# A 17-tap convolution with three outputs from five products over pairs of batches, and the last scaling of a layer norm on ScalarE

## The chip, the cores and the metric

One Trainium2 chip, one core of it. The metric is the time of one execution of the kernel on the device in microseconds, median of three runs. TensorE (PE in the rows) multiplies matrices and writes PSUM; VectorE (DVE), ScalarE (ACT) and GpSimd (POOL) work element by element; SyncE (SP) issues the transfers. Each engine takes its own instructions strictly in the order in which they are written, and they meet through semaphores.

## What is computed

Sixteen graphs (batches) of 512 nodes with 128 channels go through two layers. The first, cut to what matters here:

```
xc = x.T                                     # per batch 128 x 512
h  = relu(bn1(conv1x1(xc)))
h  = bn2(conv1d(h, conv2_w, 17 taps, padding 8))     # 128 -> 128 channels
x_conv = relu(h + xc).T
s = x @ w_se.T + b_se                        # 3 columns
A = exp(-|s_n - s_m|^2) * adj                # 512 x 512
x_nmp = A @ relu(x @ w_msg.T + b_msg)
gi = [x_conv, x_nmp] @ w_ih.T + b_ih ; gh = x @ w_hh.T + b_hh
r, z = sigmoid(gi_r + gh_r), sigmoid(gi_z + gh_z)
g  = (1 - z) * tanh(gi_n + r * gh_n) + z * x
x  = layernorm(x + g)
```

The second layer, five small graph convolutions, touches only the first 25 nodes of each batch; they are worked off together near the end.

## The kernel before

Everything is kept transposed, channels on the 128 partitions and the 512 nodes along the free side. Products that must be exact to nearly fp32 are made of three: each operand is split into a high part (`_h`, rounded by a copy on ScalarE) and a low part (`_l`, the rest, a subtraction on VectorE), and `mm3` adds high·high, high·low and low·high in PSUM.

The 17-tap convolution makes two neighbouring outputs from four products. `first_conv` writes relu(bn1(...)) into `h1`; `differences` and `sums_differences` make `dd` (528 columns) and `sd` (1056 columns) from its even and odd columns, which are split into `_h` and `_l`. `conv_part` multiplies them with the taps, grouped by three: four parts of 6, 5, 6 and 6 groups, so 23 x 3 = 69 matmuls of 256 columns for each batch, into the halves of `p_outer` and `p_middle`. ScalarE brings the middle parts to `mid`, VectorE makes `cu` from `p_outer` and the input (`outer_sum`), and then `cv` (`conv_sum`), two operations on every other column and one on all.

`first` works off batch 0 and prepares batch 1. Then come fifteen steps, written with one function `step` for each engine: batch 1, a loop of three rounds over the batches 2 to 13, and batches 14 and 15. In step b the engines finish the gates and the layer norm of batch b-1 while TensorE works on batch b. On TensorE a step is: the convolution's `p_outer` parts, in odd steps the six `rows` matmuls that serve two batches, `conv1` and `msg` of batch b+1, the first middle part, four transposes of the result of b-1, the second middle part, twelve matmuls with the masked `am` (the neighbour product), then 27 gate matmuls of 512 columns in three groups of nine: those that use x, those that use the neighbours (`n_h`, `n_l`) and those that use the convolution (`c_h`, `c_l`), with the four `dist` matmuls of b+1 put between them. `rt`, `zt` and `nn` are tanh on ScalarE; `gg`, `tt`, `ya`, `yb`, `y2` on VectorE combine them.

On VectorE the layer norm of b-1 is `stats`, `moments` (which also makes `base`), and `normalise`: one small operation for `x1`, which keeps the first nodes for the second layer, and four of 128 columns that write `yo`, (yn - mean) * rs. `rs` is a power made by GpSimd (`powers`). After `normalise` come the four `mask` operations. SyncE stores `yo` and then, in the same queue, issues the four loads of `adj` for batch b+2, and in the next step the load of `xin` for three batches ahead. `right` is filled by a transfer from `left` (`rows_left`) once for two batches.

## Time and profile before

| | us |
|---|---|
| median of 3 runs (387.93 to 392.32) | 389.65 |
| the profiled execution | 387.58 |
| its span in the trace | 385.8 |
| TensorE busy | 367.9 |
| VectorE busy | 348.9 |
| ScalarE busy | 227.6 |
| GpSimd busy | 38.9 |

The span runs from the first instruction to the last. A matmul stands in the trace from its start to the modelled end of its last column, and the next one starts meanwhile; so the distance between the starts of neighbouring matmuls is what one costs, and a full share of TensorE says little by itself. Short operations of the other engines overlap a little in the same way. An entry such as `<-ACT am_h` names what an engine waited for.

### The profile page before, as it was taken

What the parts mean: (1) busy time and instruction counts of PE and PEld (TensorE: products, weight loads), DVE (VectorE), ACT (ScalarE), POOL (GpSimd) and SP (SyncE); (2) the same over time, 40 slices, a digit from 0 to 9 for tenths busy, and PEclk for the clock granted to TensorE, in tenths of its full rate; (3) what the DMA queues carried; (4) which work ended last, traced back from release to release, by engine and by line L of the source; (5) the groups of instructions that cost most, each with busy time, mean ns of one, the idle gap of its engine ahead of it and who ended that gap; (6) DMA issues with size and microseconds to landing.
All of it is one profiled execution on the core that took longest, in us unless ns stands there. A gap on an engine that the chain in (4) does not pass through costs nothing.

```text
span 385.8 us, 7010 instructions
## 1 busy us (share of the span) xinstructions
PE 367.9 (95%) x2259; PEld 319.9 (83%) x2259; DVE 348.9 (90%) x719; ACT 227.6 (59%) x353; POOL 38.9 (10%) x54
## 2 busy tenths in 40 slices
PE   4799999999999999999999999999999999899994
PEld 2687988989797989889898979898898979687783
DVE  4998999999999999999999999999999999975746
ACT  5573756575656665655756666666657564644350
POOL 7000030100101010101001010101010060111013
PEclk9999999999999999999999999999999999999999
DMA  8662405050231405050403114050504003000100
GB/s 224 205 194 81 138 11 165 1 159 14 61 108 31 134 12 163 0 163 10 136 27 111 52 37 137 0 163 10 163 0 145 23 11 130 2 27 2 33 29 22
DMA packets 27342, 30.23 MB, mean 78 GB/s; under 512 B 3098, under 2 KB 16338, under 8 KB 27322
## 3 DMA queue, kind: packets, MB, share of 16 engines
q1 hardware_dynamic: 26860, 29.87, 25.2%
q8 instruction: 10, 0.16, 0.2%
q10 hardware_dynamic: 462, 0.12, 0.1%
q14 instruction: 10, 0.08, 0.1%
HBM read 24.84 MB, written 4.40 MB: 76 GB/s over the span
## 4 chain that ended last, share of the span: by engine, by line
PE 66%; DVE 18%; issue 9%; ACT 4%; DMA 1%; DVEq 0%; POOLq 0%; SPq 0%; ACTq 0%; POOL 0%
PE p_outer L605 14%; PE ring L605 14%; PE p_middle L605 9%; PE p_r L605 8%; PE p_z L605 7%; PE p_gi L605 7%; PE p_gh L605 5%; DVE sd_l L1134 3%; DVE st L1172 2%; DVE n_l L1210 2%; DVE sd L1130 1%; DVE sd L1129 1%; ACT rows L861 1%; DVE m_l L1143 1%; DVE dd L1120 1%
## 5 line engine op out<-in xcount | busy, mean ns | idle before, releaser
L605 PE MATMUL p_middle<-sd_h,w_h 128*128 128x256 f32 x192 | 56.8, 296 | 0.0
L605 PE MATMUL p_middle<-sd_h,w_l 128*128 128x256 f32 x192 | 54.3, 283 | 0.0
L605 PE MATMUL p_middle<-sd_l,w_h 128*128 128x256 f32 x192 | 54.0, 281 | 0.0
L1072 POOL TENSOR_TENSOR rs<-base,cst 128x5 f32<-128x5 f32 x16 | 20.0, 1249 | 325.6 <-DVE base L1183 325.6
L605 PE MATMUL p_outer<-dd_h,w_l 128*128 128x256 f32 x176 | 49.4, 281 | 0.0
L605 PE MATMUL p_outer<-dd_h,w_h 128*128 128x256 f32 x176 | 49.4, 280 | 0.0
L605 PE MATMUL p_outer<-dd_l,w_h 128*128 128x256 f32 x176 | 49.3, 280 | 0.0
L886 ACT ACTIVATE am<-ring 128x512 f32<-128x512 f32 x56 | 33.3, 595 | 19.4 <-PE ring L605 18.9
L1149 DVE TENSOR_TENSOR am<-am,adj 128x512 f32<-128x512 f32 x64 | 40.9, 683 | 1.3 <-ACT am L886 1.3
L1306 DVE TENSOR_TENSOR am_l<-am,am_h 128x2048 fp32r<-128x2048 f32 x15 | 34.4, 2292 | 3.3 <-ACT am_h L981 3.2
L605 PEld LDWEIGHTS p_middle<-sd_h,w_h 128*128 128x128 f32 x192 | 36.4, 189 | 0.3 <-issue 0.2
L605 PEld LDWEIGHTS p_middle<-sd_l,w_h 128*128 128x128 f32 x192 | 36.3, 189 | 0.2 <-issue 0.2
L605 PEld LDWEIGHTS p_middle<-sd_h,w_l 128*128 128x128 f32 x192 | 36.3, 189 | 0.0
L605 PEld LDWEIGHTS p_outer<-dd_l,w_h 128*128 128x128 f32 x176 | 33.3, 189 | 0.6
L605 PEld LDWEIGHTS p_outer<-dd_h,w_h 128*128 128x128 f32 x176 | 33.2, 189 | 0.7
L605 PEld LDWEIGHTS p_outer<-dd_h,w_l 128*128 128x128 f32 x176 | 33.1, 188 | 0.0
L605 PE MATMUL ring<-right,left 128*128 128x512 f32 x62 | 26.0, 422 | 6.1 <-DVE n_l L1210 4.1
L981 ACT ACTIVATE am_h<-am 128x2048 fp32r<-128x2048 f32 x15 | 28.5, 1902 | 0.0
L900 ACT ACTIVATE c_h<-cv 128x512 fp32r<-128x512 f32 x16 | 10.1, 633 | 24.8 <-DVE cv L1206 24.8
L605 PE MATMUL ring<-am_h,m_l 128*128 128x512 f32 x60 | 23.5, 392 | 0.0
L605 PE MATMUL ring<-am_l,m_h 128*128 128x512 f32 x60 | 23.5, 392 | 0.0
L605 PE MATMUL ring<-am_h,m_h 128*128 128x512 f32 x60 | 23.5, 392 | 0.0
(297 smaller groups left out, 959.8 us busy)
## 6 DMA issues: line engine op xcount, KB each, us to landing
adj<-adjT SPq DMA_DIRECT2D x64, 256.0 KB, 3.4
xin<-xT SPq DMA_DIRECT2D x17, 256.0 KB, 3.0
out<-yo SPq DMA_DIRECT2D x16, 256.0 KB, 2.5
gw<-g_w SPq DMA_DIRECT2D x2, 640.0 KB
wc<-w_c SPq DMA_DIRECT2D x2, 384.0 KB, 4.6
right<-left SPq DMA_DIRECT2D x15, 48.0 KB
wg<-w_ih SPq DMA_DIRECT2D x1, 384.0 KB, 5.6
wc<-w_c SPq DMA_DIRECT2D x1, 320.0 KB, 4.0
```

The source lines that it names most:

```text
L605: return nc.tensor.matmul(out_, w, x, start=start, stop=stop, skip_group_check=True)
L861: A(ab, p_gh[:], ACT.Identity, bias=rowb[:, 0:1], scale=cst[:, C_ROW:C_ROW + 1]).then_inc(s_ab, 1)
L886: A(am[:, c, :], R_D[c][:], ACT.Exp).then_inc(s_e[c], 1)
L900: A(c_h[:], cv[:], ACT.Relu).then_inc(s_ch, 1)
L981: A(am_h[:], am[:], ACT.Copy).then_inc(s_amh, 1)
L1072: TT(rs[:], base[:], cst[:, C_MH:C_MH + CH + 1], ALU.pow).then_inc(s_rs, 1)
L1120: TT(dd[:], halves(h1, 0), halves(h1, 2), ALU.subtract).then_inc(s_dd, 1)
L1134: TT(sd_l[:], sd[:], full(sd_h[:]), ALU.subtract).then_inc(s_sdl, 1)
L1149: TT(am[:, c, :], am[:, c, :], adj[:, c, :], ALU.mult).then_inc(s_am[c], 1)
L1172: last = nc.vector.bn_stats(st[:, c, :], yn[:, c, :])
L1210: TT(n_l[:], R_NMP[:], full(n_h[:]), ALU.subtract).then_inc(s_nl, 1)
L1306: TT(am_l[:], am[:], full(am_h[:]), ALU.subtract).then_inc(s_aml, 1)
```

## The change

It has two parts.

The first: each five products give three outputs, for two batches at once. `h1` holds two batches side by side. VectorE makes from it five streams of 2 x 178 columns: `neighbour_steps` (712 columns) and `second_steps` (1068) take differences, `inner` (712) makes streams 1 and 2, `outer` (712) streams 0 and 4, and stream 3 is read from the second differences directly; ScalarE copies the high parts (712, 712 and 356 columns) and VectorE subtracts the low parts (`inner_low`, `outer_low`, `middle_low`). `stream` multiplies: 6, 6, 6, 6 and 5 groups of three taps, three matmuls each, 87 matmuls of 2 x 172 = 344 columns for a pair. Two streams are multiplied in the odd step, three in the even step after it, so that odd and even steps have functions of their own. Out of PSUM, ScalarE writes `ev`; VectorE makes `pq` (`first_sums`, 2 x 344 columns, in the odd step), `vv` (`second_sums`, 3 x 344), adds the input on all three phases (`add_input`, 1026 columns with a stride of three) and two more phases of 342 columns (`add_first`, `add_last`). `c_h` and `c_l` are made for both batches at once (1024 columns). In odd steps `conv1` is done for two batches, and the convolution's gate matmuls stand before those of the neighbours. In the first batch, `first` makes both batches' streams and all five products, with a fifth set of weights, three of them sums of taps; `add_input` is spread over other operations there. Buffers are laid over one another: `t_raw` over `ya`, `yb` and `y2`, `cv` over `rt` and `zt`, `gw1` over the old taps, which is now loaded in the last step.

The second: the four operations that write `yo` move from VectorE's `normalise` to ScalarE, as Identity with a scale `rs` and a bias `nb` for each partition. GpSimd makes `nb` = -(mean * rs) with two operations more after its power. On ScalarE they stand at the end of a step, behind `gates`; in the last step ahead of them.

The diff, cut to its core; of the step functions of TensorE, ScalarE and VectorE only the new text and kept lines are shown, in that order:

```
 G3 = (TAPS + 1) // 3
-PH = HALF + PAD
+TILE3 = (N + 2) // 3
+N3 = 3 * TILE3
+NM = TILE3 + 1
+J3 = NM + G3
+W3 = 3 * J3
+XS = N3 + 1
...
+def window(t, at, g):
+    return t[:, at, :].rearrange("p (b j) -> p b j", b=2)[:, :, g:g + NM]
+def stream(k, to):
+    w_h, w_l = (w0_h, w1_h, w2_h, w3_h, w4_h)[k], (w0_l, w1_l, w2_l, w3_l, w4_l)[k]
+    at = (2, 0, 1, 4, 3)[k]
     count = w_h.shape[1]
     for g in range(count):
-        par, i = (3 * g + first) % 2, (3 * g + first) // 2
-        last = mm3(out_, w_h[:, g, :], w_l[:, g, :], v_h[:, par, i:i + HALF], v_l[:, par, i:i + HALF],
+        last = mm3(both(to, NM), w_h[:, g, :], w_l[:, g, :], window(t_h, at, g), window(t_l, at, g),
                    g == 0, g == count - 1)
-    return last
...
+    after(pe, s_t3h, n.pair(1)); after(pe, s_t3l, n.pair(1))
+    after(pe, s_ev, n.pair(1))
+    stream(3, p_outer)
+    after(pe, s_e[3], n(1))
+    msg(q, R_MSG)
+    after(pe, s_t04h, n.pair(1)); after(pe, s_t04l, n.pair(1))
+    after(pe, s_pq, n.pair(1))
+    stream(0, p_middle)
+    turn(n)
+    after(pe, s_v, n.pair(1))
+    stream(4, p_outer)
+    after(pe, s_mt, n(2))
+    neighbour_product(0, n)
+    after(pe, s_rt, n(0)); gate(p_r, "r", 2, xb_h, xb_l, True, False)
+    after(pe, s_zt, n(0)); gate(p_z, "z", 2, xb_h, xb_l, True, False)
+    after(pe, s_ghb, n(0)); gate(p_gh, "n", 2, xb_h, xb_l, True, True).then_inc(s_gx, 1)
+    after(pe, s_left, n.pair(1)); after(pe, s_right[1], n.pair(1) * 16)
+    after(pe, s_yn, n(0))
+    dist(q, 0)
+    after(pe, s_nh, n(1)); after(pe, s_nl, n(1))
+    dist(q, 1)
+    gate(p_r, "r", 1, n_h[:], n_l[:], False, False)
+    after(pe, s_e[0], n(2))
+    dist(q, 2)
+    gate(p_z, "z", 1, n_h[:], n_l[:], False, False)
+    after(pe, s_tt, n(0)); gate(p_gi, "n", 1, n_h[:], n_l[:], True, False)
+    after(pe, s_e[1], n(2))
+    dist(q, 3)
+    after(pe, s_ch, n.pair(1)); after(pe, s_cl, n.pair(1))
+    gate(p_r, "r", 0, cb_h, cb_l, False, True).then_inc(s_gr, 1)
+    gate(p_gi, "n", 0, cb_h, cb_l, False, True).then_inc(s_gi, 1)
+    gate(p_z, "z", 0, cb_h, cb_l, False, True).then_inc(s_gz, 1)
...
+    cb_h, cb_l = c_h[:, 1, :], c_l[:, 1, :]
     more = not static(b, B - 1)
     if static(b, B - 1):
+        pe.wait_ge(s_w0, PAIRS); pe.wait_ge(s_w2, PAIRS)
         g_pe.spread(pe, mm)
+    if more:
         after(pe, s_xh, n(3)); after(pe, s_xl, n(3)); after(pe, s_ghb, n(0))
         rows(v + 1)
+        after(pe, s_w0, n.pair(0)); after(pe, s_pq, n.pair(0))
+        conv1(q, p_middle)
+        after(pe, s_w2, n.pair(0))
+        conv1(r, p_outer)
         after(pe, s_e[3], n(1))
         msg(q, R_MSG)
+    after(pe, s_rt, n(0))
+    gate(p_r, "r", 2, xb_h, xb_l, True, False)
+    gate(p_r, "r", 0, cb_h, cb_l, False, False)
+    after(pe, s_zt, n(0))
+    gate(p_z, "z", 2, xb_h, xb_l, True, False)
+    gate(p_z, "z", 0, cb_h, cb_l, False, False)
+    after(pe, s_tt, n(0))
+    gate(p_gi, "n", 0, cb_h, cb_l, True, False)
     if static(b, B - 1):
         g_pe.combine(pe, mm)
+    if more:
+        after(pe, s_val, n.pair(1))
+    after(pe, s_ghb, n(0)); gate(p_gh, "n", 2, xb_h, xb_l, True, True).then_inc(s_gx, 1)
+    turn(n)
+    if more:
+        after(pe, s_mt, n(2))
     else:
+        after(pe, s_e[3], n(1))
+    neighbour_product(1, n)
     if static(b, B - 1):
         pe.wait_ge(s_msel, 2)
         pe.wait_ge(s_grow, B - 2)
         for i in EARLY:
             g_pe.aggregate(pe, mm, i)
+    if more:
+        after(pe, s_t12h, n.pair(1)); after(pe, s_t12l, n.pair(1))
+        after(pe, s_h1, n(3))
+        stream(1, p_outer)
+        after(pe, s_left, n.pair(1)); after(pe, s_right[0], n.pair(1) * 16)
         after(pe, s_yn, n(0))
         dist(q, 0)
+        stream(2, p_middle)
     after(pe, s_nh, n(1)); after(pe, s_nl, n(1))
     if more:
         dist(q, 1)
+    gate(p_r, "r", 1, n_h[:], n_l[:], False, True).then_inc(s_gr, 1)
     if more:
         after(pe, s_e[0], n(2))
         dist(q, 2)
+    gate(p_gi, "n", 1, n_h[:], n_l[:], False, True).then_inc(s_gi, 1)
     if more:
         after(pe, s_e[1], n(2))
         dist(q, 3)
+    gate(p_z, "z", 1, n_h[:], n_l[:], False, True).then_inc(s_gz, 1)
...
+def first_sum(n, source):
+    after(act, s_sum[1], n.pair(1)); after(act, s_pq, n.pair(0))
+    A(ev, both(source, NM), ACT.Identity, bias=prm[:, P_A2:P_A2 + 1], scale=prm[:, P_NH:P_NH + 1]).then_inc(s_ev, 1)
...
+def normalise(q, n, k):
+    after(act, s_nb, n(k + 1)); after(act, s_rs, n(k + 1))
+    act.wait_ge(s_out[q], dma_count(n, q, k))
+    for c in range(CH):
+        last = A(yo[q][:, c, :], yn[:, c, :], ACT.Identity, bias=nb[:, c:c + 1], scale=rs[:, c:c + 1])
+    last.then_inc(s_yo, 1)
...
+def even(b, v, n):
+    if before(b, B - 2):
+        x_high(v, n, 2)
+    candidate(n, -1)
+    mask_high(n)
+    msg_high(1, n, 1)
+    node_rows(n, -1)
+    if before(b, B - 2):
+        x_high(v, n, 3)
+    neighbours(n)
+    conv_out(n)
+    exps(n, 1, 0)
+    gate_n(n)
+    for c in range(1, CH):
+        exps(n, 1, c)
+    gates(n)
+    normalise(1, n, -1)
+def odd(b, v, n):
+    more = not static(b, B - 1)
+    candidate(n, -1)
+    if more:
         rows_factor(n, 0)
+    mask_high(n)
+    if more:
+        first_conv(n, 1, 0, p_middle)
+        first_conv(n, 2, 1, p_outer)
         rows_high(n, 0)
+        msg_high(0, n, 1)
+    else:
         g_act.combined(act)
     node_rows(n, -1)
+    gate_n(n)
+    if more:
+        inner_high(n)
+    neighbours(n)
+    if more:
+        middle_high(n)
+        exps(n, 1, 0)
+        first_sum(n, p_outer)
+        outer_high(n)
+        for c in range(1, CH):
+            exps(n, 1, c)
+    else:
         act.wait_ge(s_ya, B - 1)
         for i in EARLY:
             g_act.channels(act, i)
+        normalise(0, n, -1)
     gates(n)
+    if more:
+        normalise(0, n, -1)
...
     after(pool, s_base, n(k + 1))
     after(pool, s_yo, n(k))
+    after(pool, s_grow, n(k))
     TT(rs[:], base[:], cst[:, C_MH:C_MH + CH + 1], ALU.pow).then_inc(s_rs, 1)
+    after(pool, s_mv, n(k + 1)); after(pool, s_rs, n(k + 1)); after(pool, s_nb, n(k))
+    TT(nmr[:], mv[:, :, 0], rs[:, 0:CH], ALU.mult).then_inc(s_nmr, 1)
+    after(pool, s_nmr, n(k + 1))
+    TT(nb[:], nmr[:], minus[:], ALU.mult).then_inc(s_nb, 1)
...
+def neighbour_steps(n):
+    after(dve, s_h1, n(3)); after(dve, s_t3h, n.pair(0)); after(dve, s_t3l, n.pair(0))
+    TT(phases(ef, 0)[:, 1:3], phases(hh, 1)[:, 1:3], phases(hh, 0)[:, 1:3], ALU.subtract).then_inc(s_steps, 1)
+def inner(n):
+    after(dve, s_steps, n.pair(1)); after(dve, s_t12h, n.pair(0)); after(dve, s_t12l, n.pair(0)); after(dve, s_y2, n(0))
+    STT(t_raw[:, 0:2], he[:, :, 1:2 * W3:3], -2.0, phases(ef, 0)[:, 2].unsqueeze(1).broadcast_to([128, 2, 2 * J3]),
+        ALU.mult, ALU.add).then_inc(s_t12, 1)
+def inner_low(n):
+    after(dve, s_t12h, n.pair(1)); after(dve, s_sum[1], n.pair(0)); after(dve, s_sum[2], n.pair(0))
+    TT(t_l[:, 0:2], t_raw[:, 0:2], full(t_h[:, 0:2]), ALU.subtract).then_inc(s_t12l, 1)
+def second_steps(n):
+    after(dve, s_h1, n(3)); after(dve, s_t12, n.pair(1))
+    TT(ef[:, 0:2 * W3], hh[:, 0:2 * W3], hh[:, 2:2 * W3 + 2], ALU.subtract).then_inc(s_f, 1)
+def outer(n):
+    after(dve, s_f, n.pair(1)); after(dve, s_t04h, n.pair(0)); after(dve, s_t04l, n.pair(0)); after(dve, s_t, n(0))
+    STT(t_raw[:, 2:4], phases(ef, 0)[:, 0:2], 2.0, phases(ef, 0)[:, 1:3], ALU.mult, ALU.subtract).then_inc(s_t04, 1)
+def outer_low(n):
+    after(dve, s_t04h, n.pair(1)); after(dve, s_sum[0], n.pair(0)); after(dve, s_sum[4], n.pair(0))
+    TT(t_l[:, 2:4], t_raw[:, 2:4], full(t_h[:, 2:4]), ALU.subtract).then_inc(s_t04l, 1)
+def middle_low(n):
+    after(dve, s_t3h, n.pair(1)); after(dve, s_sum[3], n.pair(0))
+    TT(t_l[:, 4], phases(ef, 0)[:, 1], full(t_h[:, 4]), ALU.subtract).then_inc(s_t3l, 1)
...
+def first_sums(n, source):
+    after(dve, s_sum[2], n.pair(1)); after(dve, s_ev, n.pair(1)); after(dve, s_v, n.pair(0)); after(dve, s_cx, n.pair(0))
+    STT(pq[:, 0], both(source, NM), prm[:, P_N6:P_N6 + 1], ev, ALU.mult, ALU.add)
+    STT(pq[:, 1], both(source, NM), prm[:, P_P6:P_P6 + 1], ev, ALU.mult, ALU.add).then_inc(s_pq, 1)
+def second_sums(n):
+    after(dve, s_sum[3], n.pair(1)); after(dve, s_pq, n.pair(1)); after(dve, s_cx, n.pair(0))
+    STT(vv[:, 0], both(p_outer, NM), prm[:, P_N6:P_N6 + 1], pq[:, 0], ALU.mult, ALU.add)
+    STT(vv[:, 1], both(p_outer, NM), prm[:, P_N3:P_N3 + 1], pq[:, 1], ALU.mult, ALU.add)
+    STT(vv[:, 2], both(p_outer, NM), prm[:, P_N23:P_N23 + 1], pq[:, 0], ALU.mult, ALU.add).then_inc(s_v, 1)
+def add_input(v, n):
+    after(dve, s_v, n.pair(1)); after(dve, s_yb, n(0)); after(dve, s_gg, n(0))
+    at = v % 4
+    TT(cv[:, :, 0:N3].rearrange("p b (i k) -> p k b i", k=3), vv[:, :, :, 0:TILE3],
+       xpad[:, at:at + 2, 0:N3].rearrange("p b (i k) -> p k b i", k=3), ALU.add).then_inc(s_cx, 1)
+def add_first(n):
+    after(dve, s_sum[0], n.pair(1)); after(dve, s_cx, n.pair(1))
+    STT(tiles(cv, 0), both(p_middle, TILE3), prm[:, P_H2:P_H2 + 1], tiles(cv, 0), ALU.mult, ALU.add).then_inc(s_w0, 1)
+def add_last(n):
+    after(dve, s_sum[4], n.pair(1)); after(dve, s_cx, n.pair(1))
+    STT(tiles(cv, 2), both(p_outer, TILE3), prm[:, P_S2:P_S2 + 1], tiles(cv, 2), ALU.mult, ALU.add).then_inc(s_w2, 1)
...
+def even(b, v, n):
+    gate_mid(n, -1)
+    keep_share(v, n, -1, n.pair(1))
+    if before(b, B - 2):
+        x_low(v, n, 2)
+    result(n, -1)
+    second_sums(n)
+    msg_sum(n, 1, R_MSG)
+    mask_low(n)
+    add_input(v, n)
+    add_first(n)
+    stats(n, -1)
+    msg_low(1, n, 1)
+    add_last(n)
+    moments(n, -1)
+    if before(b, B - 2):
+        x_low(v, n, 3)
+    neighbours_low(n)
+    conv_low(n)
+    normalise(1, n, -1, pair_of(b, v))
+    for c in range(CH):
+        mask(n, 1, c)
+def odd(b, v, n):
     more = not static(b, B - 1)
     gate_mid(n, -1)
     keep_share(v, n, -1)
+    if more:
+        rows_val(n, 0)
     result(n, -1)
+    if not more:
         g_dve.columns(dve)
+    mask_low(n)
+    if more:
+        msg_sum(n, 1, R_MSG)
+        neighbour_steps(n)
+        inner(n)
+        second_steps(n)
+        inner_low(n)
+        rows_left(n, 0)
+    else:
         g_dve.prepare(dve)
     stats(n, -1)
     if more:
+        outer(n)
+        msg_low(0, n, 1)
     moments(n, -1)
+    if more:
+        middle_low(n)
     neighbours_low(n)
+    if more:
+        outer_low(n)
+    normalise(0, n, -1, pair_of(b, v))
+    if more:
+        first_sums(n, p_middle)
         for c in range(CH):
             mask(n, 1, c)
```

VectorE's order in `first` of the changed kernel is: small weights and `x_low`, `second_steps`, low part of w0, `outer`, `rows_val`, `outer_low`, low part of w4, `rows_left`, `right`, `msg_sum`, the two operations for w3's sum, `middle_low`, one for w2's, `neighbour_steps`, w1's sum, low part of w3, `inner`, w2's sum, two masks, the first phase from stream 0, low part of w1, `inner_low`, the last phase from stream 4, low part of w2, two masks, two for `sel1`, `msg_sum`, three phases from stream 3, low part of `wg`, `x_low` twice, `msg_low`, two for `ac`, `first_sums`, three additions, `neighbours_low`, `conv_low`. TensorE multiplies stream 0, four `dist`, stream 4, `msg`, small selections, and then streams 3 (which waits for the first phase), 1 and 2 (which waits for the three phases from stream 3), and the neighbour product.

## Rows read from the trace of the kernel before

**Rows 1.** the page, part 1: busy us (share), instructions

```profile
PE 367.9 (95%) x2259; PEld 319.9 (83%) x2259; DVE 348.9 (90%) x719; ACT 227.6 (59%) x353; POOL 38.9 (10%) x54
```

**Rows 2.** timeline, VectorE, first operation of each step: start us, duration us, instruction

```profile
40.24 0.69 DVE L1153 SCALAR_TENSOR_TENSOR gg<-rt,gg 128x512 f32<-128x512 f32 x1
...
167.50 0.69 DVE L1153 SCALAR_TENSOR_TENSOR gg<-rt,gg 128x512 f32<-128x512 f32 x1
...
189.65 0.69 DVE L1153 SCALAR_TENSOR_TENSOR gg<-rt,gg 128x512 f32<-128x512 f32 x1
...
210.10 0.69 DVE L1153 SCALAR_TENSOR_TENSOR gg<-rt,gg 128x512 f32<-128x512 f32 x1
...
319.24 0.67 DVE L1153 SCALAR_TENSOR_TENSOR gg<-rt,gg 128x512 f32<-128x512 f32 x1
...
339.38 0.69 DVE L1153 SCALAR_TENSOR_TENSOR gg<-rt,gg 128x512 f32<-128x512 f32 x1
...
362.08 0.69 DVE L1153 SCALAR_TENSOR_TENSOR gg<-rt,gg 128x512 f32<-128x512 f32 x1 [2.40 <-ACT rt L912]
```

**Rows 3.** timeline, TensorE, one step of an even batch

```profile
153.10 0.28 PE L605 MATMUL p_middle<-sd_l,w_h 128*128 128x256 f32 x1
...
155.00 0.29 PE L605 MATMUL p_middle<-sd_h,w_l 128*128 128x256 f32 x1
...
157.70 0.39 PE L605 MATMUL ring<-am_h,m_h 128*128 128x512 f32 x1
...
160.22 0.39 PE L605 MATMUL ring<-am_h,m_l 128*128 128x512 f32 x1
```

**Rows 4.** groups, TensorE, moving operand in seven pieces: count, busy us, mean ns

```profile
L605 PE MATMUL p_outer<-xin,gw 128*128 128x350 f32 x2 | 0.8, 460 | 0.0
```

**Rows 5.** timeline, VectorE, operations of the same stretch

```profile
196.55 0.48 DVE L1199 SCALAR_TENSOR_TENSOR cu<-p_outer,prm,xin 128x256 f32<-128x256 f32 x1
...
197.53 0.70 DVE L1120 TENSOR_TENSOR dd<-h 128x528 f32<-128x528 f32 x1
...
198.15 0.71 DVE L1129 TENSOR_TENSOR sd<-h 128x528 f32<-128x528 f32 x1
...
203.51 1.25 DVE L1134 TENSOR_TENSOR sd_l<-sd,sd_h 128x1056 fp32r<-128x1056 f32 x1
...
206.47 1.12 DVE L1193 TENSOR_SCALAR yo<-yn,mv,rs 128x128 f32<-128x128 f32 x4
```

**Rows 6.** groups, ScalarE, by form

```profile
L981 ACT ACTIVATE am_h<-am 128x2048 fp32r<-128x2048 f32 x15 | 28.5, 1902 | 0.0
...
L900 ACT ACTIVATE c_h<-cv 128x512 fp32r<-128x512 f32 x16 | 10.1, 633 | 24.8 <-DVE cv L1206 24.8
...
L869 ACT ACTIVATE h<-ring,prm 128x512 f32<-128x512 f32 x16 | 12.4, 775 | 7.5 <-PE ring L605 7.5
```

**Rows 7.** timeline, ScalarE, beginning of a step

```profile
190.29 0.69 ACT L914 ACTIVATE zt<-p_z,prm 128x512 f32<-128x512 f32 x1 [0.67 <-PE p_z L605]
...
190.87 0.62 ACT L857 ACTIVATE x_h<-xin 128x512 fp32r<-128x512 f32 x1
```

**Rows 8.** timeline, VectorE and TensorE, waits in two steps

```profile
185.19 0.47 PE L605 MATMUL ring<-right,left 128*128 128x512 f32 x1 [0.36 <-DVE n_l L1210]
...
193.94 2.29 DVE L1306 TENSOR_TENSOR am_l<-am,am_h 128x2048 fp32r<-128x2048 f32 x1 [0.25 <-ACT am_h L981]
```

**Rows 9.** timeline, VectorE and GpSimd, near 313 us

```profile
312.39 1.96 DVE L1214 SCALAR_TENSOR_TENSOR c_l<-cv,c_h 128x512 fp32r<-128x512 f32 x1
...
313.75 2.05 POOL L1084 TENSOR_TENSOR ac<-ac,dinv 106x848 f32<-106x848 f32 x1
```

**Rows 10.** timeline, VectorE and TensorE, end of the first batch

```profile
30.77 0.60 DVE L1276 TENSOR_TENSOR ac<-p_gi,cst 106x424 f32<-106x424 f32 x1 [0.17 <-PE p_gi L605]
...
34.70 0.69 DVE L1210 TENSOR_TENSOR n_l<-ring,n_h 128x512 fp32r<-128x512 f32 x1 [1.18 <-ACT n_h L904]
...
40.50 0.28 PE L605 MATMUL p_outer<-dd_h,w_h 128*128 128x256 f32 x1
```

509 lines of the change are left out of this document (237 added, 272 removed).

## The prediction

> **What bounds the kernel now.** I read the page's shares first. TensorE and VectorE both stand above 90% [rows 1], so no engine can be called the bound from there, and the next views are the starts of the steps and the waits within them. The operation `gg` opens each step on VectorE [rows 2]. An odd step, with the `rows` matmuls, takes 189.65 - 167.50 = 22.15 us, an even one 210.10 - 189.65 = 20.45, the pair 42.60. A matmul of 256 columns costs (155.00 - 153.10)/16 = 0.1185 us, one of 512 columns (160.22 - 157.70)/11 = 0.229 [rows 3]; the gates run at about 0.233. Summing a pair of steps on TensorE: 138 convolution matmuls 16.35, 24 for the neighbours 5.5, 54 gates 12.6, 18 of 512 columns for `conv1`, `rows` and `dist` and the small ones about 7: some 41.5. TensorE is idle for one us of 42.6, and one such place is its wait for `n_l` [rows 8]. VectorE reaches 41 us of work too, with a wait for `am_h` that is 0.25 us long [rows 8]. So TensorE sets the pace and VectorE follows less than 4% behind. Whatever is taken from TensorE pays only as far as VectorE's and ScalarE's chains let it.
>
> **TensorE's gain.** Between the two prices of rows 3, 344 columns cost 0.1185 + 88 x 0.00044 = 0.157 us. The operand now comes in two pieces; one of 350 columns in seven pieces lasts 460 ns [rows 4], nothing beyond its length, so I add nothing. Per pair 87 x 0.157 = 13.65 instead of 16.35: 2.7 us less, 21.5 over eight pairs. A pair would take TensorE 38.8: odd 19.6, even 19.2.
>
> **VectorE's work.** An operation of N columns costs its start-to-start distance, 0.62 for 528 [rows 5], and with the 1.25 for 1056 that is N/0.96 + 0.07. With PSUM as a source 256 columns are 0.48 long [rows 5], 0.40 start to start, so 344 are 0.49. Stride two cost nothing against contiguous (`dd` 0.70); stride three has no row, and I take it as free; bound: 1.5 times as long, 0.25 to 0.4 us for each of the seven large strided operations, 2 us a pair.
> Out, per pair: `dd` and `sd` 3.7, their low parts 3.75, `outer_sum` 1.6, `conv_sum` 2.8, two `conv_low` 1.2, `yo` 2 x 1.04 [rows 5]: 15.1. In: 712 columns four times 3.25, 1068 1.2, 356 0.45, `first_sums` 1.0, `second_sums` 1.45, `add_input` 1.15, two phases 1.0, `conv_low` of 1024 1.15, waits on its own results 0.7: 11.35. VectorE falls by 3.7 to about 38, but unevenly: some 20.4 in the odd step, 17.6 in the even one. The odd step now asks more of VectorE than of TensorE.
>
> **ScalarE's part.** The sum hardly moves; the order does. The four `yo` operations stand between `zt` of one step and `nn` of the next. A copy of 512 columns lasts 633 ns, of 2048 1902, so 0.826 ns a column; `h`, which also has bias and scale per partition, lasts 775 at 512 columns [rows 6]. At 128 columns that is 0.32 to 0.46 us, and the next operation starts 0.1 early (190.29 + 0.69 against 190.87 [rows 7]): 0.22 to 0.36 each, up to 0.41 as the source is SBUF. I take 0.36, as both operands are there: 1.45 us for four, ends 0.9 and 1.6. In the old kernel they were 1.04 us in VectorE's queue, with nobody waiting but the masks behind them.
> The Trainium skill, page "ScalarE: Activation LUTs", section "What ACT_TABLE_LOAD costs", gives 186 ns plus 0.833 ns per element plus 93 ns for each pointer operand, less a 93 ns overlap: an estimate of 0.386 us each, 1.55 for four, by which each step would be 0.1 us later. The rows above agree in slope (0.826), and the sum goes by them.
>
> **A walk through an odd step,** time 0 at the end of TensorE's previous step; each figure is the end of an operation, from the costs above. `zt` starts 0.2, then `yo`; `nn` can start at 2.25 and `rows_factor` gives `ab` at 3.65. VectorE has `gg`, `tt`, `ya` done at 1.6, and its next is `rows_val`, which was behind `am_l` before and now waits for `ab`: 2.0 us idle, with everything below queued behind it. Then `rows_val` 4.35, `yb`, `y2` 5.75, `am_l` 7.95, `msg_sum` 8.55, `neighbour_steps` 9.35, `inner` 10.3, `second_steps` 11.6, `inner_low` 12.4, `rows_left` 13.05, `n_l` 16.95. TensorE: `rows` 1.4, two `conv1` 2.8, `msg` 3.6, five gate groups and `gh` 7.8, transposes 8.2, then 0.5 idle for `mt`, neighbours 11.45; stream 1 waits until 12.5 for `inner_low`, ends 15.3; `dist` waits 0.3 for the transfer out of `left`; stream 2 ends 18.7, the rest 21.5. So 21.5 against 22.15, where 19.6 would be its own work. VectorE ends at 22.5 with the masks, and `gg` follows within 0.3.
> **An even step:** `zt` 1.3, `yo` to 2.65, `x_h` 3.3, for which `x_low` waits 0.6, `yb`, `y2` 5.3, `second_sums` 6.8, `msg_sum` 7.4, `am_l` 9.6. TensorE is through streams 3, 0, 4 at 9.3, waits 0.45, neighbours 12.5, gates 14.85, waits for `n_l` until 15.35 (`add_input`, `add_first`, `stats`, `msg_low`, `add_last`, `moments`, `x_low` stand ahead of it), end 20.55. Before: 20.45.
> The pair is 42.05 against 42.6. From step 1 to step 14 the old kernel took 319.24 - 40.24 = 279.0 [rows 2]. The new one: 7 x 21.5 + 6 x 20.55 = 273.8, and 2.0 more in step 13, where `c_l` lasts 1.96 us [rows 9] instead of some 0.7 while GpSimd works on large tiles, and the next operation is as much longer; that stays. Together 275.8: -3.2.
>
> **The first batch** pays for both. The first difference waits for a second `conv1`: 9.4 instead of 7.65 us. VectorE works more: differences and low parts for two batches, one more weight sum and low part, about 4.7 us of `cv`; by the same costs stream 3 starts when the first phase is out of `p_outer`, at 27.2, stream 2 at 34.6 behind the phases from stream 3, ending 37.4; neighbour product 3.0, `dist` 0.7, the selections 0.8, so `ac` at 42.2 instead of 30.77, `n_l` at 45.75 instead of 34.70 [rows 10], and step 1 starts on TensorE at 51.7 instead of 40.50 [rows 10]: +11.2. Bounds: +8, if `ac` and the phases overlap better; +14, if TensorE starts again more slowly after its idle times of three us, which I have no row for.
> **The last two steps.** Step 14 has streams but no preparation of x: 0.5 less than its 20.14. Step 15 took 362.08 - 339.38 = 22.7 [rows 2] and has no convolution: spread, five gate groups, `combine`, neighbours behind `am_l` (8.1), aggregates, the rest: 15.1, so -7.6; but ScalarE has `yo` ahead of `gates` there, 1.45 us, of which 1.0 reaches `nn` and the tail. -6.6, bounds -4 and -8.
> `yo` after the end of the last batch stands in an idle stretch of ScalarE: nothing. GpSimd's two small operations end long before `yo` needs them; nothing. The store and four `adj` loads behind it on SyncE start 3 us later into the next step and are wanted 15 us after; nothing, but if that cover went, each us late would stop the masks for one.
> Sum: +11.2 - 3.2 - 0.5 - 6.6 = +0.9 on 385.8, so 386.7, and the execution 1.8 more, 388.5. The profiled execution (387.58) lies 0.5% under the median of 389.65, so as a median it is 390.5.
>
> **Rivals.** *TensorE keeps its pace.* If ScalarE's four operations cost 0.25 and the waits of the walk are absorbed, the pair goes to TensorE's own 38.8 plus the old kernel's small gaps, 39.6: 6.5 x (42.05 - 39.6) = 16 us less, 374; half of it gives 382. For it: TensorE's old steps show hardly any wait; against: the 2.0 us at `rows_val` cannot be hidden, as a queue has no way around.
> *VectorE's strided operations are slower,* place: odd step from `neighbour_steps` to `inner_low`. There every us goes through stream 1 to the end of the step. It decides from 0.65 us a step, when the odd step passes 22.15. At 1.5 times the length, 1.3 us in the odd step and 0.5 in the even one, 6.5 x 1.8 = 12 more, with 2 in the first batch: 404; at a third of that 395. For: no row has stride three; against: stride two is free.
> *GpSimd beside VectorE.* The stretch near 313 us costs `c_l` 1.3 us [rows 9]; two more GpSimd operations a step of four columns could cost 0.2 each: +6, 396. The Trainium skill, "GPSIMD Engine Reference", section "1. Specifications", says that the SBUF interfaces are shared with VectorE when it reads two SBUF inputs; rows 9 agree for large tiles, and whether small ones suffer is what this rival asks.
> *The products don't get cheaper:* two pieces cost as much as a second start, 87 matmuls at 0.19. The gain of 2.7 a pair is gone; in the walk 1.2 of it comes back in either step, 2.4 a pair, 6.5 x 2.4 = 16 and 2 in the first batch: 406.
>
> **Chances.** My sum (384 to 394) 0.40; TensorE's pace, in full or half, 0.33; strided VectorE 0.15; GpSimd 0.08; products 0.04. Runs of the same kernel differ by 1%, so that is what can be told from no change, 385.8 to 393.5. A quarter of my sum's runs would lie outside one per cent on the slow side or the fast one; together faster is 0.34, same 0.38, slower 0.28. The range leaves out a tenth on either side: 375 to 402; mine alone 384 to 394.
>
> **What would show it.** Convolution matmuls 0.157 apart. `rows_val` waits 2 us for ScalarE; stream 1 waits about 1 us for `inner_low`; the pair at 42; `gg` of step 1 at 51 to 52; step 15 near 15. I am wrong if the pair falls below 41, if strided operations of 712 columns last over 0.9 us, or if step 1 starts before 48.

## The result, and the profile after

The changed kernel takes 397.3 us (median of 4 runs, 396.6 to 399.5), beside 391.0 us for the kernel before on the same chip (387.9 to 392.8): ratio 1.018, interval 1.010 to 1.026. It is slower; whether by more or less than 2% the interval leaves open. The profiled execution has a span of 395.5 us against 385.8, so the 9.7 us between the two traces are what has to be found. The clock granted to TensorE was 0.993 over the whole run, 0.999 in the kernel before; run 7 asks what that difference costs.

The page of the changed kernel, part 1, against [rows 1]:

```profile
PE 355.2 (90%) x1851; PEld 301.7 (76%) x1851; DVE 333.6 (84%) x612; ACT 230.1 (58%) x378; POOL 53.4 (14%) x92
```

TensorE is 12.7 us less busy and VectorE 15.3 us less, and yet the span has grown. Both shares fell: no engine is as near to its limit as before, which is how time lost in waits between engines looks.

The rows carry the names of the shared buffers: `gtn` holds `gg`, `tt` and `nn`; `rz` holds `rt`, `zt` and then `cv`; `yy` holds `ya`, `yb`, `y2` and the raw streams; `he` holds `h1` and the differences; `wc` holds `ev`, `pq` and `vv`; `rows` holds `ab` (written by `rows_factor` on ScalarE) and the result of `rows_val`; `yoo` holds `yo`. The first operation (`gg`) of some steps on VectorE, against [rows 2]:

```profile
54.50 0.68 DVE L1286 SCALAR_TENSOR_TENSOR gtn<-rz,gtn 128x512 f32<-128x512 f32 x1
...
183.14 0.69 DVE L1286 SCALAR_TENSOR_TENSOR gtn<-rz,gtn 128x512 f32<-128x512 f32 x1
...
206.49 0.68 DVE L1286 SCALAR_TENSOR_TENSOR gtn<-rz,gtn 128x512 f32<-128x512 f32 x1
...
226.05 0.69 DVE L1286 SCALAR_TENSOR_TENSOR gtn<-rz,gtn 128x512 f32<-128x512 f32 x1
...
338.00 0.68 DVE L1286 SCALAR_TENSOR_TENSOR gtn<-rz,gtn 128x512 f32<-128x512 f32 x1
...
371.80 0.69 DVE L1286 SCALAR_TENSOR_TENSOR gtn<-rz,gtn 128x512 f32<-128x512 f32 x1 [2.75 <-ACT rz L987]
```

Split at the same places as [rows 2]: the first batch ends at 54.50 instead of 40.24, +14.3 us. Steps 1 to 13 take 338.00 - 54.50 = 283.5 instead of 279.0, +4.5. Steps 14 and 15 take 33.8 instead of 42.8, -9.0. What follows takes 23.7 in both. Sum +9.7. A pair of steps is 23.35 + 19.56 = 42.9 us, against 42.6. So more than half of the loss, 5.2 us, arises outside steps 1 to 13, in the first batch and the last two steps.

TensorE's saving is there in full. The second and the last of the 18 matmuls of stream 1, in the odd step that begins at 183 us:

```profile
197.02 0.32 PE L640 MATMUL p_outer<-t_l,w_h 128*128 128x344 f32 x1
...
199.60 0.32 PE L640 MATMUL p_outer<-t_h,w_l 128*128 128x344 f32 x1
```

16 starts further in 2.58 us, 0.161 apart. In the windows of steps 2 to 12, TensorE is busy for 219.8 of 235.5 us (93%), where the old kernel had 231.2 of 233.0 (99%), and VectorE for 211.3. Neither is the bound by its sum; the order of VectorE's queue in the odd step is. Timeline of that step, ScalarE, VectorE and one row of TensorE:

```profile
184.40 1.65 ACT L1053 ACTIVATE yoo<-yn,nb,rs 128x128 f32<-128x128 f32 x4
185.94 0.72 ACT L993 ACTIVATE gtn<-gtn,vec 128x512 f32<-128x512 f32 x1
186.56 0.77 ACT L933 ACTIVATE rows<-p_gh,rowb,cst 128x512 f32<-128x512 f32 x1
...
187.36 0.75 DVE L1231 SCALAR_TENSOR_TENSOR rows<-p_gh,brow,rows 128x512 f32<-128x512 f32 x1 [2.12 <-ACT rows L933]
...
192.21 1.13 DVE L1240 TENSOR_TENSOR he<-he 128x712 f32<-128x712 f32 x1
193.37 1.12 DVE L1245 SCALAR_TENSOR_TENSOR yy<-he 128x712 f32<-128x712 f32 x1
194.60 1.27 DVE L1254 TENSOR_TENSOR he<-he 128x1068 f32<-128x1068 f32 x1
195.79 0.89 DVE L1250 TENSOR_TENSOR t_l<-yy,t_h 128x712 fp32r<-128x712 f32 x1
...
196.79 0.40 PE L640 MATMUL p_outer<-t_h,w_h 128*128 128x344 f32 x1 [1.43 <-issue]
```

Three things are to be seen. VectorE stands for 2.12 us at `rows_val` until `yo`, `nn` and `ab` are through ScalarE. From then on it has no gap up to `inner_low`, and TensorE is idle for 1.43 us ahead of stream 1. The row names no releaser (`issue`), but `inner_low` ends at 196.68 and the matmul starts at 196.79. And two operations of the same 712 columns last 1.13 and 0.89 us: the first has its columns three apart, the second has them side by side.

### The profile page after: what moved, and what is told of

Read it like the earlier page. It is cut to its first block and busy times, and to the rows that moved or that the text cites. A ratio compares the mean times of both kernels' runs of the same rounds, so it can differ in the third digit from the quotient of the medians.

```text
span 395.5 us, 6216 instructions
## 1 busy us (share of the span) xinstructions
PE 355.2 (90%) x1851; PEld 301.7 (76%) x1851; DVE 333.6 (84%) x612; ACT 230.1 (58%) x378; POOL 53.4 (14%) x92
## 5 line engine op out<-in xcount | busy, mean ns | idle before, releaser
L640 PE MATMUL p_outer<-t_h,w_h 128*128 128x344 f32 x137 | 46.1, 337 | 16.8 <-issue 12.3
L640 PE MATMUL p_outer<-t_h,w_l 128*128 128x344 f32 x137 | 44.7, 327 | 0.0
L640 PE MATMUL p_outer<-t_l,w_h 128*128 128x344 f32 x137 | 44.7, 326 | 0.0
L640 PEld LDWEIGHTS p_outer<-t_h,w_h 128*128 128x128 f32 x137 | 26.3, 192 | 20.8 <-issue 19.5
L640 PE MATMUL p_middle<-t_h,w_h 128*128 128x344 f32 x95 | 31.2, 328 | 0.0
L640 PE MATMUL p_middle<-t_l,w_h 128*128 128x344 f32 x95 | 30.6, 322 | 0.0
L640 PE MATMUL p_middle<-t_h,w_l 128*128 128x344 f32 x95 | 30.5, 321 | 0.0
L640 PEld LDWEIGHTS p_outer<-t_l,w_h 128*128 128x128 f32 x137 | 26.4, 193 | 0.3
L640 PEld LDWEIGHTS p_outer<-t_h,w_l 128*128 128x128 f32 x137 | 26.5, 193 | 0.0
L1053 ACT ACTIVATE yoo<-yn,nb,rs 128x128 f32<-128x128 f32 x64 | 26.3, 491 | 0.0
```

The costliest lines, as they stand in the source:

```text
L640: return nc.tensor.matmul(out_, w, x, start=start, stop=stop, skip_group_check=True)
L1053: last = A(yo[q][:, c, :], yn[:, c, :], ACT.Identity, bias=nb[:, c:c + 1], scale=rs[:, c:c + 1])
```

## The experiments

Theory 1, held from here on: the pace is set by VectorE's queue in the odd step, through the wait at `rows_val` and the length of the strided operations, and by the same queue in the first batch. The rivals: GpSimd's small operations slow VectorE; TensorE sets the pace in either kernel; in the first batch TensorE's lower clock does. Each ratio is to the kernel before, in runs on the same chip; the range in brackets behind it is its 95% interval.

**1. The first part of the change alone.**

```diff
 # VectorE, normalise, behind x1, ahead of the masks
+                dve.wait_ge(s_out[q], dma_count(n, q, k))
+                for c in range(CH):
+                    last = TS(yo[q][:, c, :], yn[:, c, :], mv[:, c, 0:1], rs[:, c:c + 1], ALU.subtract, ALU.mult)
 # ScalarE: normalise(q, n, -1) out;  GpSimd: nmr, nb out
```

> The changed kernel with yo back on VectorE (four operations, 1.04 us, ahead of the masks) and without GpSimd's two small ones; the convolution in three phases stays. It is the first part of the change alone. Theory 1, the queues: in the odd step VectorE's 2.1 us of idle at rows_val go, 1.0 us of yo comes in, so the odd step falls from 23.3 to about 22.2, the even one stays near 19.8, the pair at 42.0; steps 1 to 13 276 to 278 us instead of 283.5, the whole 388 to 392, the ratio to the kernel before about 1.00. Rival, the convolution itself is what made the kernel slower and yo's place costs nothing: the pair stays at 42.9 and the ratio at 1.018, or above it, as VectorE has more to do.

Ratio 1.012 (1.007 to 1.017), 393.7 us. The odd step takes 23.04 us, not 22.2, the even one 19.30, the pair 42.34, steps 1 to 13 281.9 us, not 276 to 278; time and ratio came out above what was expected too. The miss is in the wait, which doesn't go altogether:

```profile
186.18 0.75 DVE L1215 SCALAR_TENSOR_TENSOR rows<-p_gh,brow,rows 128x512 f32<-128x512 f32 x1 [0.86 <-ACT rows L933]
```

`ab` stands behind `nn`, and `nn` behind `tt`, which takes longer than VectorE's `ya`. So the wait falls by 1.26 us and `yo` brings 1.04 back. The first part costs 1.2% by itself. The second adds about 0.6% to it by the two ratios, which their intervals don't separate from nothing; by the traces it adds 0.57 us to a pair of steps (42.91 against 42.34).

**2. The second part alone, on the kernel before.**

```diff
 # ScalarE, end of each step of the kernel before
                 gates(n)
+                normalise(q, n, -1)
 # GpSimd: nmr and nb behind rs;  VectorE: the four operations of yo out
```

> The kernel before with the second part of the change alone: yo on ScalarE behind the gates of each step, the shift on GpSimd. Theory 1: nn and am_h start 1.5 us later in every step, the copy am_h was waited for already, so am_l and the neighbour product come 1.2 to 1.5 us later, and VectorE's 1.04 us less does not give it back, as TensorE waits: step pair 44.5 to 45.5 instead of 42.5, the whole 403 to 412, ratio 1.035 to 1.055. Rival, the second part is harmless or a gain in the kernel before, and only the two parts together meet: 386 to 392, ratio 0.99 to 1.005.

Ratio 1.045 (1.041 to 1.050), 405.7 us; the pair 45.25 instead of 42.6. Within the expectation, but the main wait stands elsewhere than I had it:

```profile
202.06 0.69 DVE L1121 TENSOR_TENSOR x_l<-xin,x_h 128x512 fp32r<-128x512 f32 x1 [1.36 <-ACT x_h L857]
...
204.48 2.29 DVE L1316 TENSOR_TENSOR am_l<-am,am_h 128x2048 fp32r<-128x2048 f32 x1 [0.33 <-ACT am_h L988]
...
216.15 0.47 PE L605 MATMUL ring<-right,left 128*128 128x512 f32 x1 [1.60 <-DVE n_l L1220]
```

`x_high` opened ScalarE's part of every step, and VectorE's `x_low` now waits 1.36 us for it. Everything behind it in VectorE's queue is as much later, and it comes out at `n_l`, for which TensorE waits 16.1 us in 11 steps, 1.5 in each (the view of waits from 63 to 311 us); in the kernel before it was 1.4 us in all. The second part is the same in both kernels and costs 4.5% in the one and about 0.6% in the other.

**3. `yo` in an idle place.** All operations of the changed kernel, another order.

```diff
 # ScalarE, even step                      # ScalarE, odd step
                 mask_high(n)                              rows_high(n, 0)
+                normalise(0, n, -2)       +               normalise(1, n, -2)
                 msg_high(1, n, 1)                         msg_high(0, n, 1)
 # end of either step: normalise(q, n, -1) out
 # SyncE: load_adj(b + 1, ...), x load, store(b - 2, ...) in this order
```

> The changed kernel with all its operations, but yo of a batch stands one step later in ScalarE's queue: in an even step behind the copy am_h, in an odd one behind val_h, in both ahead of yn. SyncE's queue is turned so that the adj and x loads stand ahead of the store. Theory 1: rows_val no longer waits, every odd step is 1.8 to 2.1 us shorter, 21.3, the pair 40.8 to 41.2, steps 1 to 13 269 to 272, the whole 381 to 386, ratio 0.975 to 0.985. Rival, TensorE or GpSimd sets the step and the wait only moves to another place: the pair stays above 42.5, ratio 1.01 to 1.02.

Ratio 0.992 (0.988 to 0.995), 385.8 us, 2.6% less than the changed kernel by the two ratios. The odd step is 22.03, the even one 18.92, the pair 40.95. The expectation held for the pair and the time; it missed the odd step by 0.7 and the ratio (0.975 to 0.985 expected), for the reason of run 1: 0.80 us of the wait at `rows_val` are left. The even step is 0.64 shorter, 0.51 of it the wait of `x_low` for ScalarE, which is gone. SyncE's queue was turned in the same run, and no run separates the two; but in steps 2 to 12 no wait of VectorE names a transfer, in the changed kernel or here, and the waits that went are those for ScalarE. So the place of `yo` is shown as a cause, with 1.95 us a pair.

**4. Columns side by side.**

```diff
-                TT(phases(ef, 0)[:, 1:3], phases(hh, 1)[:, 1:3], phases(hh, 0)[:, 1:3], ALU.subtract)
+                TT(ef[:, 0:4 * J3], hh[:, 1:1 + 4 * J3], hh[:, 0:4 * J3], ALU.subtract)
 # likewise inner, outer, middle_low, add_input; tiles(t, k) gives t[:, :, k * TILE3:(k + 1) * TILE3]
```

> The changed kernel with all VectorE operations of stride three on contiguous columns of the same number (neighbour_steps, inner, outer, middle_low, add_input, add_first, add_last, and those of the first batch); the convolution's values are not those of the reference. Theory 1: 712 columns fall from 1.12 to 0.90 us, add_input from 1.57 to 1.2, phases from 0.67 to 0.56; 0.45 us of it lies ahead of stream 1 and 0.7 in the odd step's queue, 0.6 in the even one's; the pair falls by 0.7 to 1.3 to about 41.9, the whole to 388 to 392, ratio 0.995 to 1.005. Rival, stride costs nothing and the 1.12 us come from the SBUF ports shared with GpSimd or from the length alone: the operations stay at 1.12 and the ratio at 1.018.

Ratio 0.996 (0.993 to 0.998), 387.9 us; its convolution computes something else, only the lengths are of use. Groups of VectorE in steps 2 to 12, first the changed kernel, then this one (mean ns of one behind the bar):

```profile
L1342 DVE TENSOR_TENSOR rz<-wc,xpad 128x1026 f32<-128x1026 f32 x6 | 9.4, 1566 | 0.0
...
L1240 DVE TENSOR_TENSOR he<-he 128x712 f32<-128x712 f32 x5 | 5.6, 1129 | 0.0
...
L1347 DVE SCALAR_TENSOR_TENSOR rz<-p_middle,prm,rz 128x342 f32<-128x342 f32 x6 | 4.0, 674 | 0.6
```

```profile
L1342 DVE TENSOR_TENSOR rz<-wc,xpad 128x1026 f32<-128x1026 f32 x6 | 7.3, 1222 | 0.0
...
L1240 DVE TENSOR_TENSOR he<-he 128x712 f32<-128x712 f32 x5 | 4.5, 893 | 0.0
...
L1347 DVE SCALAR_TENSOR_TENSOR rz<-p_middle,prm,rz 128x342 f32<-128x342 f32 x6 | 3.5, 576 | 0.6
```

1129 against 893 ns: stride three makes the operation 26% longer. The pair is 22.85 + 19.01 = 41.86, steps 1 to 13 take 277.1, 6.4 less, and the first batch is 1.0 shorter (run 7). Without the stride the changed kernel would have drawn level with the old one.

**5. GpSimd without its two small operations.**

```diff
 # GpSimd: nmr and nb out
-                    last = A(yo[q][:, c, :], yn[:, c, :], ACT.Identity, bias=nb[:, c:c + 1], scale=rs[:, c:c + 1])
+                    last = A(yo[q][:, c, :], yn[:, c, :], ACT.Identity, bias=minus[:, c:c + 1], scale=rs[:, c:c + 1])
```

> The changed kernel without GpSimd's two small operations (nmr and nb); yo takes a constant as its shift, so the mean is not taken out of the output. Theory 1, the queues: VectorE's operations keep their lengths, the pair of steps stays at 42.9, the whole within 1 us of the changed kernel. Rival, GpSimd beside VectorE: the operations of VectorE around base and middle_low get shorter, 0.2 us for each of the two left out, 0.8 us a pair, 5 us in all, pair 42.1.

Ratio 1.022 (1.014 to 1.030), 396.4 us. The pair that begins at 182 us is 23.32 + 19.50 = 42.8, within 0.1 of the changed kernel's; `neighbour_steps` lasts 1130 ns as before, `am_l` 2284. This rival is out for small operations. For large ones it stays as [rows 9] have it, and the loss falls on other operations as the order changes. Step 13 of the changed kernel, VectorE and GpSimd:

```profile
332.69 1.62 POOL L1202 TENSOR_TENSOR he<-cst,dinv 106x848 f32<-106x848 f32 x1
...
332.96 5.11 DVE L1282 TENSOR_TENSOR am<-am,adj 128x512 f32<-128x512 f32 x4
...
334.27 2.05 POOL L1204 TENSOR_TENSOR ac<-ac,dinv 106x848 f32<-106x848 f32 x1
```

Four masks take 5.11 us instead of 2.48, so step 13 is 25.96 us long instead of 23.35: the same kind of loss as in the old kernel, now on the masks instead of `c_l`. In run 6, below, the same GpSimd operations met the masks differently:

```profile
327.28 4.82 POOL L1202 TENSOR_TENSOR he<-cst,dinv 106x848 f32<-106x848 f32 x1
...
327.54 2.48 DVE L1282 TENSOR_TENSOR am<-am,adj 128x512 f32<-128x512 f32 x4
...
331.26 1.38 DVE L1295 SCALAR_TENSOR_TENSOR yy<-rz,xpad 128x512 f32<-128x512 f32 x1
...
332.06 2.05 POOL L1204 TENSOR_TENSOR ac<-ac,dinv 106x848 f32<-106x848 f32 x1
...
332.57 2.09 DVE L1299 SCALAR_TENSOR_TENSOR yy<-rz,gtn 128x512 f32<-128x512 f32 x1
```

There the masks keep their 2.48 us and GpSimd's operation stretches from 1.62 to 4.82, so step 13 is 23.21 us; the loss comes in step 14, where `ya` takes 1.38 and `yb` 2.09 us instead of 0.68, 2.1 us in all. The loss moves from one step to the next, it does not go.

**6. Fewer matmuls.**

```diff
-                    last = mm3(both(to, NM), w_h[:, g, :], w_l[:, g, :], window(t_h, at, g), window(t_l, at, g), ...)
+                    mm(both(to, NM), w_h[:, g, :], window(t_h, at, g), g == 0, False)
+                    last = mm(both(to, NM), w_h[:, g, :], window(t_l, at, g), False, g == count - 1)
```

> The changed kernel with two instead of three products in every matmul group of the convolution's five streams (the one with the low part of the weights is left out, 16 matmuls in the odd step, 13 in the even one); its output is less exact. Theory 1: TensorE gets 2.5 us less in an odd step and 2.05 in an even one, but VectorE's queue sets both, and what it can give back are its waits for the exponentials, 0.5 us in either step: pair 41.7 to 42.4, the whole 389 to 394. Rival, TensorE sets the pace and the waits are only shifted about: pair 38.4, the whole 366 to 370.

Ratio 1.008 (1.002 to 1.013), 391.4 us. With 29 matmuls less a pair, 4.6 us of TensorE, the pair is 23.26 + 18.96 = 42.2: 0.7 us came out. TensorE gives away what it is spared and waits longer: from 76 us to the end of step 12 it is busy for 87% instead of 93%. Its granted clock over the whole run is lower (0.969 against 0.993), but in this pair it is 1.00, as in the changed kernel's, so that is not what took the gain. Of all the runs this one says most directly what bounds the new kernel: not TensorE.

**7. The first batch: order, and a filled gap.**

```diff
 # run 7a, VectorE, first()                # run 7b, TensorE, first()
                 x_low(0, z, 0)                            msg(0, FIRST_MSG)
+                x_low(0, z, 1)            +               for _ in range(12):
                 dve.wait_ge(s_wrowd, 16)  +                   mm(p_gi[:], wc1_h[:], x_h[0][:])
```

> The changed kernel with one edit in the first batch: x_l of batch 1 stands ahead of the split of wrow on VectorE, which waits 1.2 us for its transfer. Theory 1: the second conv1 and h follow 1.2 us earlier, and as VectorE's queue carries the first batch, gg of step 1 starts 0.8 to 1.3 us earlier, at 53.2 to 53.7 instead of 54.50. Rival, TensorE's lower clock or the weights' transfers set the first batch: gg of step 1 within 0.3 of 54.50.

> The changed kernel with 12 matmuls of 512 columns into a free bank between msg and stream 0 of the first batch, where TensorE was idle for 2.95 us; their result is not used. Theory of the clock: with no idle time ahead of it stream 0 runs at 0.158 us a matmul from its start instead of 0.287 for 14 of them, ends 1.8 us earlier, and gg of step 1 comes 1.0 to 1.8 us earlier. Theory 1: stream 0 ends earlier but stream 3 waits for the phase on VectorE as before (29.68), and gg of step 1 stays within 0.4 of 54.50.

One run each, 395.1 and 395.5 us. `gg` of step 1 stands at 52.62 in the one and at 53.26 in the other, but in run 5, whose first batch is unchanged, at 53.18: the 1.2 us wait for `wrow`'s transfer differs from run to run (none in run 5, 1.61 in run 6). Both expectations took 54.50 as the mark and missed by that. So I measure from VectorE's first difference, `second_steps`, on. Its row and that of `gg`, for the changed kernel, run 5, run 7a and run 7b:

```profile
10.89 1.27 DVE L1382 TENSOR_TENSOR he<-he 128x1068 f32<-128x1068 f32 x1 [2.43 <-ACT he L941]
```

```profile
9.59 1.27 DVE L1378 TENSOR_TENSOR he<-he 128x1068 f32<-128x1068 f32 x1 [2.14 <-ACT he L941]
...
53.18 0.69 DVE L1282 SCALAR_TENSOR_TENSOR gtn<-rz,gtn 128x512 f32<-128x512 f32 x1
```

```profile
9.01 1.27 DVE L1382 TENSOR_TENSOR he<-he 128x1068 f32<-128x1068 f32 x1 [0.76 <-ACT he L941]
...
52.62 0.69 DVE L1286 SCALAR_TENSOR_TENSOR gtn<-rz,gtn 128x512 f32<-128x512 f32 x1
```

```profile
9.58 1.27 DVE L1384 TENSOR_TENSOR he<-he 128x1068 f32<-128x1068 f32 x1 [2.20 <-ACT he L943]
...
53.26 0.69 DVE L1288 SCALAR_TENSOR_TENSOR gtn<-rz,gtn 128x512 f32<-128x512 f32 x1
```

43.61, 43.59, 43.61 and 43.68 us: the first batch is one chain behind that operation. With the columns side by side it is 42.58 (run 4). In the changed kernel VectorE has no wait at all between 15.59 and 39.57 us; from there the end hangs on TensorE, whose streams 3 and 2 waited 2.03 and 1.66 us for VectorE's phases, and on `ac`, for which VectorE waits 4.80 us. Run 7a therefore saves the wait for `wrow` where there is one, and 0.6 us where there is none. Run 7b did not do what it was meant for: the 12 matmuls ended at 14.07, TensorE was idle for 1.88 us more, and then ran at the granted clock of 0.50, the 1.2 GHz level, with matmuls 0.287 apart instead of 0.16, as in the changed kernel. It still says something. Its clock fell a second time near 30 us, where ten matmuls of stream 3 stood 0.287 apart, 1.3 us lost on TensorE; the first batch became 0.07 to 0.09 us longer. There the clock costs next to nothing that the end sees. For stream 0 itself no run lifted the clock; that VectorE waits for nothing in that stretch is the evidence there.

**8. The three reorderings together, and what stride three still costs.**

```diff
 # run 3's order and run 7a's, and in VectorE's odd step
+                result(n, -1)
                 if more:
                     rows_val(n, 0)
-                result(n, -1)
```

> The changed kernel with three reorderings: yo one step later on ScalarE as in the run that moved it, the result (yb, y2) ahead of rows_val in the odd step, and x_l of batch 1 ahead of wrow in the first batch. Theory 1: the 0.80 us that VectorE still waited for ab fall to 0.1, the odd step goes from 22.0 to 21.3, the even one stays at 19.0, the first batch is 0.5 to 1.8 shorter; 6.5 us less than with yo moved alone, 378 to 382, ratio 0.968 to 0.980. Rival, TensorE's own 19.6 plus its waits for stream 1 already set the odd step: odd step at 21.9 or above, 384 to 386.

Ratio 0.986 (0.982 to 0.989), 383.1 us: the fastest kernel of the study with the reference's computation, 3.2% less than the changed kernel by the ratios. The pair is 21.81 + 18.94 = 40.75, only 0.2 less than in run 3, because the copy of the masks is next in line:

```profile
180.03 0.75 DVE L1234 SCALAR_TENSOR_TENSOR rows<-p_gh,brow,rows 128x512 f32<-128x512 f32 x1
181.11 2.29 DVE L1470 TENSOR_TENSOR am_l<-am,am_h 128x2048 fp32r<-128x2048 f32 x1 [0.33 <-ACT am_h L1062]
```

Of the 0.80 us at `rows_val` 0.33 are now at `am_l`. So the expected 21.3 was again wrong in not asking what is late next, and 383.1 us lies between the 378 to 382 expected and the rival's 384 to 386. TensorE is busy for 217.1 of 224.5 us here, 97%, so it is itself close to setting the pace.

> The same three reorderings and, on top, all VectorE operations of stride three on contiguous columns of the same number (the convolution's values are not those of the reference). It asks what stride three still costs once the queue's waits are gone. Theory 1: VectorE's queue is still the bound, so the 1.0 us a pair that contiguous columns saved in the changed kernel are saved here too: pair 39.3 instead of 40.3, 7 to 9 us less than the reorderings alone. Rival, TensorE takes over as the bound (38.8 a pair by its own work and its small gaps): 2 to 4 us less.

Ratio 0.964 (0.960 to 0.967), 375.0 us, 8 us less; the pair 21.52 + 18.41 = 39.9, 0.8 less than with the stride. At 39.9 it is 1.1 above TensorE's own 38.8 of the prediction. In this kernel too the convolution's values are not the reference's.

**9. The stride by itself.** Operations on `am` and `adj` behind the last one of the kernel.

```diff
+            for out_, a_, b_ in forms:
+                for _ in range(2):
+                    dve.wait_ge(s_probe, count)
+                    TT(out_, a_, b_, ALU.subtract).then_inc(s_probe, 1)
+                    count += 1
```

> The changed kernel with 18 VectorE subtractions of 672 fp32 columns behind its last operation, two of each form, each waiting for the one ahead; nobody reads them. Forms in order: contiguous; contiguous in two pieces of 336; both inputs of stride two; both inputs of stride three; one input of stride three; output alone of stride three; output alone of stride two; all of stride three; all in two pieces of stride three. Theory 1, the distance of the columns: 0.77 us contiguous, 0.77 with stride two, 0.95 to 1.0 us where any operand has stride three. Rival, the number of pieces or the shape of the operand: the form in two contiguous pieces is longer too, and stride three in one piece is 0.77 us.

Seven of the forms, in this order: contiguous; both inputs of stride two (its two rows); both inputs of stride three; one input of stride three; output of stride three; output of stride two; all of stride three.

```profile
397.64 0.86 DVE L1590 TENSOR_TENSOR am<-adj 128x672 f32<-128x672 f32 x1
...
401.21 0.86 DVE L1590 TENSOR_TENSOR am<-adj 128x672 f32<-128x672 f32 x1
402.10 0.86 DVE L1590 TENSOR_TENSOR am<-adj 128x672 f32<-128x672 f32 x1
...
404.08 1.04 DVE L1590 TENSOR_TENSOR am<-adj 128x672 f32<-128x672 f32 x1
...
406.23 1.05 DVE L1590 TENSOR_TENSOR am<-adj 128x672 f32<-128x672 f32 x1
...
408.41 1.05 DVE L1590 TENSOR_TENSOR am<-adj 128x672 f32<-128x672 f32 x1
...
410.39 0.86 DVE L1590 TENSOR_TENSOR am<-adj 128x672 f32<-128x672 f32 x1
...
412.40 1.07 DVE L1590 TENSOR_TENSOR am<-adj 128x672 f32<-128x672 f32 x1
```

0.86 us contiguous and with stride two, in two contiguous pieces too (starts at 399.42, 400.32 and 401.21, 0.9 apart as before), 1.05 us as soon as one operand has stride three, 1.07 with all of them and 1.05 in two such pieces (start at 414.60). I had expected 0.77 and 0.95 to 1.0, start to start; the starts are 0.89 and 1.08 apart, so both were 0.1 too low and the difference held. The distance of the columns costs, once, whichever operand has it; the number of pieces does not.

**10. Does `yo` on ScalarE pay in the kernel before, if well placed?**

```diff
 # kernel before with run 2's edit; ScalarE, each step
                 A(am_h[:], am[:], ACT.Copy).then_inc(s_amh, 1)
+                if p: normalise(1, n, -2)
 ...
                     first_conv(n, 1)
+                if not p: normalise(0, n, -2)
 # end of the step: normalise(q, n, -1) out; SyncE as in run 3
```

> The kernel before with yo on ScalarE as in the run that cost 4.5%, but one step later in its queue: behind the copy am_h in an odd step, behind h in an even one, where ScalarE was idle; SyncE's queue is turned as in the changed kernel's reordering. Theory 1: only the place of yo cost those 4.5%, and TensorE sets the old kernel's pace, so VectorE's 1.04 us less a step bring hardly anything: pair 42.2 to 42.6, ratio 0.99 to 1.005. Rival, ScalarE's four operations or GpSimd's two cost by being there: pair above 43.5, ratio over 1.02. Second rival, VectorE was the old kernel's bound as much as TensorE: pair 41.0 to 41.5, ratio 0.96 to 0.975.

Ratio 0.999 (0.996 to 1.002), 388.1 us; the pair 22.15 + 20.46, the same as [rows 2] to 0.01. The 4.5% of run 2 came with the place of `yo` (SyncE's order changed along, and neither kernel's VectorE waits for a transfer in these steps), and taking 1.04 us a step from VectorE brings nothing where TensorE sets the pace.

## Why the prediction came out as it did

The time, 397.3, lies in the range (375 to 402), but not in that of my likeliest case (384 to 394). What happened is the second rival, "VectorE's strided operations are slower", which I gave 0.15 and priced at 404 for operations half as long again, and at 395 for a third of that loss (17% longer). Measured are 26% at 712 columns, for which those prices give about 398. The sign that I had named, over 0.9 us for 712 columns, came true with 1.13. The steps, in the prediction's order:

- *TensorE's gain*: right. 0.157 us a matmul, 0.158 to 0.161 measured, and the rival "the products don't get cheaper" is out. (Its terms give 408 on the 390.5 from which the other rivals start, not 406.)
- *VectorE's work*: here is the step that failed. "Stride three has no row, and I take it as free", on the ground that stride two is free. The contiguous lengths held (`t_l` 0.89, `am_l` 2.28), though my sum counts four operations of 712 columns where a pair has five (0.8 us, so VectorE falls by 2.9 and not 3.7 before any stride; the walk through the steps has all five). Stride adds 0.22 to 0.24 us to each of three operations of 712 columns, 0.34 to `add_input`, 0.1 to each of three shorter ones: 1.3 us a pair, of which 1.05 reached the pair (run 4), 6.4 us over steps 1 to 13. My sum of -3.2 for these steps with the 6.4 of the stride is +3.2; measured +4.5. Of the 1.3 left, 0.9 are in step 5 (24.24 us instead of 23.35), where TensorE waited 0.65 us for the transfer `right`, and 0.6 are in step 13, where GpSimd's large tiles cost 2.6 us instead of 2.0. Seen on TensorE, as the walk was, the odd step took 22.04 us (21.5 forecast) and the even one 20.86 (20.55). The Trainium skill, page "Advanced Engine Details and Errata", section "SBUF Cachelines", has 16-byte lines and asks for at least two hits on a line to hide the access; two fp32 columns of stride two fall on each line, of stride three four columns fall on three. Runs 4 and 9 agree with it in where the loss begins (stride two free, stride three 22 to 26% at 672 and 712 columns); they don't show the lines themselves. I had not weighed that rule, and it speaks against this change; the page gives no size for the loss.
- *ScalarE's part*: right in place and nearly in size. Four `yo` take 1.65 us, a mean of 491 ns each, and the next operation starts 1.54 after the first: 0.385 each, where I took 0.36. The Trainium skill, page "ScalarE: Activation LUTs", section "What ACT_TABLE_LOAD costs", gave an estimate of 0.386, and the trace agrees with it to 1 ns. The wait at `rows_val` was forecast as 2.0 us and is 2.12, neighbours and stream 1 start 8.7 and 13.2 us after TensorE's last matmul of the step before (forecast 8.7 and 12.5; most of the 0.7 are the 0.46 that stride adds to `neighbour_steps` and `inner`).
- *The first batch*: +14.3 instead of +11.2, 0.3 above the upper bound of +14, for other reasons than the one named there. Behind the first difference 43.6 instead of 42.0 us: 1.0 is stride (run 4), the other 0.6 was not traced. The difference itself came 1.5 later, 1.2 of it a late transfer of `wrow` that the profiled execution happened to have. The bound's reason, that TensorE starts more slowly after its idle times, did occur (0.50 granted) and cost nothing that run 7 could find.
- *The last two steps*: -9.0 instead of -7.1. Step 14 took 17.99 us where I had 19.64, 1.57 less than the other even steps of 19.56. I took 0.5 off for the missing preparation of x, which is TensorE's view of it; but VectorE sets the pace, and there the two `x_low` and the wait ahead of the first cost 0.6 + 0.6 + 0.5 us in the even step that begins at 206.49. No run tested this by itself. The loss beside GpSimd's tiles does not come back: run 6, with 23.21 and 20.20 us for steps 13 and 14, has it in step 14 (run 5's rows).
- *GpSimd*: small operations cost nothing (run 5), large ones 2.6 us once, where I had taken 2.0.
- *TensorE keeps its pace*: rightly doubted, with the reason given, that a queue has no way around. Run 6 shows it from the other side. Half of its gain (priced at 382) was in reach by order alone, 383.1 us; the whole (priced at 374) only with contiguous columns as well, 375.0, in a kernel that does not compute the reference.

In my expectations of runs 1, 3 and 8 one mistake returns: a wait was counted as gone when its longest cause was moved, though a second cause stood 0.3 to 0.9 us behind it.

## What to carry to other kernels

Before an algorithm is changed to save matmuls, price its new operands by stride on the engine that must prepare them: here 2.7 us a pair saved on TensorE were outweighed by 1.05 us of stride and 2 us of queue order. Price its beginning and end too: the first batch and the last two steps together (+5.2 us) cost more than the thirteen steps between them (+4.5). When an operation is moved to an idle engine, look for the place in that engine's queue where nobody waits, not for the engine's share of busy time: the same four operations cost 4.5%, about 0.6% or nothing in one order or another. And price a removed wait against the next thing that is late.

## What the runs showed of the hardware

- VectorE, fp32: stride two is free (0.86 us at 672 columns, as contiguous), stride three makes the operation 17 to 28% longer (0.86 to 1.05 us at 672 columns, 0.89 to 1.13 at 712, 1.22 to 1.57 at 1026, and 0.58 to 0.67 at 342 with a PSUM source beside it), once, whether on an input or on the output. Strides above three were not run.
- Two GpSimd operations of 128x4 columns beside VectorE cost it nothing; two of 106x848 beside four operations of 512 columns made these take 5.11 instead of 2.48 us. Which engine waits can differ: in run 6 the same four kept 2.48 us, and GpSimd's first operation took 4.82 instead of 1.62.
- In run 7b TensorE worked without a gap from 7.1 to 14.1 us, the last 3.0 us on the extra matmuls, and stood idle for 1.9 us; behind that the granted clock was 0.50, with matmuls of 344 columns 0.287 us apart instead of 0.16.
